# Units of TensorE with the same array shape side by side within each round of the first and last part

## The reference

```python
xs = jnp.fft.rfft2(x, axes=(1, 2)).reshape(B, H, W // 2 + 1, 8, 48)
xr, xi = jnp.real(xs), jnp.imag(xs)
o1r = relu(einsum('bxyhi,hio->bxyho', xr, w1[0]) - einsum(xi, w1[1]) + b1[0])
o1i = relu(einsum(xi, w1[0]) + einsum(xr, w1[1]) + b1[1])
o2r = einsum(o1r, w2[0]) - einsum(o1i, w2[1]) + b2[0]
o2i = einsum(o1i, w2[0]) + einsum(o1r, w2[1]) + b2[1]
out = irfft2(softshrink(o2r, 0.01) + 1j * softshrink(o2i, 0.01)) + x
```

## Time and profile before

| | |
|---|---|
| median of 3 runs | 995.19 us (990.65 to 997.57) |
| profiled execution, own time | 993.3 us |
| its span | 991.3 us |
| TensorE busy (matmul) | 916.0 us, 92% |
| VectorE busy | 577.1 us, 58% |
| ScalarE busy | 475.8 us, 48% |
| DMA | 184.41 MB, mean 186 GB/s |
| mean granted clock of TensorE | 0.976 |

### The profile page before, as it was taken

How to read it: one execution, slowest core, us unless ns; L and a number is a source line. 1 busy time by engine, 2 the same in 40 slices (tenths; PEclk the granted TensorE clock), 3 DMA queues, 4 the chain that set the end, 5 groups by cost and what they waited for, 6 DMA issues and landing times.

```text
span 991.3 us, 14302 instructions
## 1 busy us (share of the span) xinstructions
PE 916.0 (92%) x5168; PEld 460.3 (46%) x5168; DVE 577.1 (58%) x869; ACT 475.8 (48%) x757; POOL 81.1 (8%) x157
## 2 busy tenths in 40 slices
PE   2799999999999988999999999999999999999933
PEld 1555555665676655444444434444444444444411
DVE  1255555455454765787775676666666666666511
ACT  2455444444545424434343445565655656666521
POOL 3011111011111110000000101000000000000001
PEclk8899999999999999999999999999999999999986
DMA  9879699469648979856143443343654474554463
GB/s 283 324 206 298 202 282 366 150 180 283 248 136 269 260 237 277 210 138 164 48 114 95 112 127 108 108 123 113 213 170 129 153 247 134 161 156 153 142 192 128
DMA packets 95703, 184.41 MB, mean 186 GB/s; under 512 B 13007, under 2 KB 73769, under 8 KB 93842
## 3 DMA queue, kind: packets, MB, share of 16 engines
q1 hardware_dynamic: 85490, 143.65, 48.0%
q0 software_dynamic: 9696, 39.56, 12.4%
q10 hardware_dynamic: 448, 0.30, 0.1%
HBM read 104.32 MB, written 79.14 MB: 185 GB/s over the span
## 4 chain that ended last, share of the span: by engine, by line
PE 82%; DMA 9%; SPq 2%; DVE 2%; ACT 2%; issue 1%; POOL 0%; ACTq 0%; DVEq 0%
PE psum L948 17%; PE psum L957 16%; PE psum L987 8%; PE psum L1041 6%; PE psum L1065 6%; PE psum L1025 6%; DMA RG<-rows_along_h 6%; PE psum L936 5%; PE psum L967 5%; PE psum L998 4%; PE psum L1052 3%; PE psum L913 3%; PE psum L1014 2%; DMA rows_along_h<-RD 1%; SPq L611 1%
## 5 line engine op out<-in xcount | busy, mean ns | idle before, releaser
L1374 DVE SCALAR_TENSOR_TENSOR RA<-psum,RA 112x896 f32<-112x896 f32 (+1 forms) x120 | 124.1, 1035 | 206.3 <-ACT RA L1222 205.9
L1222 ACT ACTIVATE RA<-psum,small 112x896 f32<-112x896 f32 (+1 forms) x120 | 115.7, 964 | 94.7 <-PE psum L957 94.7
L957 PE MATMUL psum<-RA,RW 112*64 112x448 f32 (+1 forms) x640 | 131.1, 531 | 1.4 <-ACT RA L1213 1.4
L1213 ACT ACTIVATE RA<-psum,RW 112x448 f32<-112x448 f32 (+1 forms) x160 | 89.2, 609 | 80.0 <-PE psum L948 80.0
L1334 DVE COPY RD<-psum 128x672 f32<-128x672 f32 (+2 forms) x122 | 69.5, 571 | 58.3 <-PE psum L987 56.8
L987 PE MATMUL psum<-RD,const 128*128 128x384 f32 (+1 forms) x304 | 98.3, 445 | 3.7 <-DVE RD L1334 2.7
L1207 ACT ACTIVATE RA<-psum 128x384 f32<-128x384 f32 (+2 forms) x72 | 50.6, 702 | 78.9 <-PE psum L936 52.6
L936 PE MATMUL psum<-const,RX 128*112 128x128 f32 x528 | 68.5, 282 | 17.1 <-DMA RX<-rows_along_w 17.1
L1359 DVE TENSOR_TENSOR RX<-RX,RA 112x768 f32<-112x768 f32 (+2 forms) x80 | 80.8, 1011 | 2.5
L1207 ACT ACTIVATE RD<-psum 128x384 f32<-128x384 f32 (+2 forms) x122 | 64.0, 525 | 32.9 <-PE psum L987 30.9
L936 PEld LDWEIGHTS psum<-const,RX 128*112 128x112 f32 x528 | 61.2, 180 | 35.7 <-issue 34.9
(11 more groups left out here) (103 smaller groups left out, 1070.1 us busy)
## 6 DMA issues: line engine op xcount, KB each, us to landing
RG<-rows_along_h SPq DMA_DIRECT2D x7, 3072.0 KB, 11.5
RX<-x SPq DMA_DIRECT2D x16, 768.0 KB, 8.6
rows_along_w<-RX SPq DMA_DIRECT2D x54, 224.0 KB, 5.1
rows_along_h<-RD SPq DMA_DIRECT2D x84, 144.0 KB, 3.3
rows_along_h<-RD SPq DMA_DIRECT2D x56, 168.0 KB, 2.9
out<-RA POOLq DMA_DIRECT2D x12, 768.0 KB, 4.0
RX<-rows_along_w SPq DMA_DIRECT2D x12, 672.0 KB, 6.5
spectrum<-RA POOLq DMA_DIRECT2D x48, 168.0 KB, 4.7
```

Source lines behind the costliest of these rows:

```text
L957: mm = nc.tensor.matmul(bank[b * HALF:(b + 1) * HALF, a * BANK:a * BANK + nk * H], w4[layer][0:ROWS, g, b, a], hidden(slot)[0:ROWS, b * N: ...
L1213: done = nc.scalar.activation(hidden(slot)[0:ROWS, b * N:b * N + nk * H], banks(key)[0:ROWS, b, 0:nk * H], ACT.Relu, bias=bias[layer][0:RO ...
L1222: nc.scalar.activation(dst, src, ACT.Relu, bias=minus_lambda_l0 if key[0] == "S4" else minus_lambda).then_inc(act_emptied, 1)
L1374: nc.vector.scalar_tensor_tensor(out=dst, in0=src, scalar=LAMBDA / 64 if key[0] == "S4" else LAMBDA, in1=dst, op0=ALU.add, op1=ALU.min).th ...
```

## The change

Within each round of `order()` the units are put in another order, so that those of one kind are neighbours. Nothing else in the file is changed: the same 637 units, the same rounds (except `CI` of the last two items, one round earlier), the same DMA code.

- A, a round before: `S2 TA [S1] [6A] S3 5A S4 [S1] [6A]`; after: `S2 TA [6A 6A] 5A [S1 S1] S3 S4`.
- C, a round before: `3L2 5C 3L3 4L2 [6C] 4L3 TC [6C]`; after: `3L2 3L3 4L2 4L3 TC 5C [6C or 6C 6C]`.
- C, the `CI` units: `3L2(0) 4L2(0) 3L2(1) CI(8,0) 4L2(1) CI(8,1) 3L2(2) CI(9,0) 3L3(0) ...` before; `3L2(0) CI(8,0) CI(8,1) 4L2(0) 3L2(1) 4L2(1) CI(9,0) 3L2(2) 3L3(0) ...` after.

```diff
@@ -110,24 +110,18 @@
             o += [("S2", r)]
         if 0 <= r - 4 < ALL_STEPS:
             o += [("TA", r - 4)]
+        for p in range(PASSES - 1):
+            if 0 <= r - flip_round(p) < FLIP_UNITS:
+                o += [("6A", p, g, r - flip_round(p)) for g in range(PASS_PAIRS)]
+        if 0 <= r - 6 < 2 * ALL_GROUPS:
+            o += [("5A", (r - 6) // 2, (r - 6) % 2)]
         for p in range(1, PASSES):
             if 0 <= r - first_transform_round(p) < X_PARTS:
-                o += [("S1", p, 2 * (r - first_transform_round(p)))]
-        for p in range(PASSES - 1):
-            if 0 <= r - flip_round(p) < FLIP_UNITS:
-                o += [("6A", p, 0, r - flip_round(p))]
+                o += [("S1", p, 2 * (r - first_transform_round(p)) + v) for v in range(2)]
         if 0 <= r - 1 < ALL_STEPS:
             o += [("S3", r - 1)]
-        if 0 <= r - 6 < 2 * ALL_GROUPS:
-            o += [("5A", (r - 6) // 2, (r - 6) % 2)]
         if 0 <= r - 2 < ALL_STEPS:
             o += [("S4", r - 2)]
-        for p in range(1, PASSES):
-            if 0 <= r - first_transform_round(p) < X_PARTS:
-                o += [("S1", p, 2 * (r - first_transform_round(p)) + 1)]
-        for p in range(PASSES - 1):
-            if 0 <= r - flip_round(p) < FLIP_UNITS:
-                o += [("6A", p, 1, r - flip_round(p))]
         if r == PREP_ROUND:
             o += [("PR",)]
         if 0 <= r - ALL_STEPS - 4 < 2:
@@ -156,27 +150,23 @@
     for r in range(C_ROUNDS):
         if r < ALL_STEPS:
             o += [("3L2", r)]
-        if r == 1:
-            o += [("CI", ITEMS - 2, 0)]
-        elif r in (2, 3):
-            o += [("CI", ITEMS - 1, r - 2)]
+        if 0 <= r - L3_LAG < ALL_STEPS:
+            o += [("3L3", r - L3_LAG)]
+        if r == 0:
+            o += [("CI", ITEMS - 2, h) for h in range(2)]
+        if r < ALL_STEPS:
+            o += [("4L2", r)]
+        if 0 <= r - L3_LAG < ALL_STEPS:
+            o += [("4L3", r - L3_LAG)]
+        if r in (1, 2):
+            o += [("CI", ITEMS - 1, r - 1)]
+        if 0 <= r - L3_LAG - 1 < ALL_STEPS:
+            o += [("TC", r - L3_LAG - 1)]
         if 0 <= r - L3_LAG - 3 < 2 * ALL_GROUPS:
             o += [("5C", (r - L3_LAG - 3) // 2, (r - L3_LAG - 3) % 2)]
-        if 0 <= r - L3_LAG < ALL_STEPS:
-            o += [("3L3", r - L3_LAG)]
-        if r < ALL_STEPS:
-            o += [("4L2", r)]
-        if r == 1:
-            o += [("CI", ITEMS - 2, 1)]
         for p in range(PASSES - 1):
             if 0 <= r - last_inverse_round(p) < S1_UNITS // inverse_rate(p):
-                o += [("6C", p, inverse_rate(p) * (r - last_inverse_round(p)))]
-        if 0 <= r - L3_LAG < ALL_STEPS:
-            o += [("4L3", r - L3_LAG)]
-        if 0 <= r - L3_LAG - 1 < ALL_STEPS:
-            o += [("TC", r - L3_LAG - 1)]
-        if 0 <= r - last_inverse_round(PASSES - 2) < S1_UNITS // 2:
-            o += [("6C", PASSES - 2, 2 * (r - last_inverse_round(PASSES - 2)) + 1)]
+                o += [("6C", p, inverse_rate(p) * (r - last_inverse_round(p)) + v) for v in range(inverse_rate(p))]
     o += [("6C", PASSES - 1, v) for v in range(S1_UNITS)]
     return o
 
```

## The result

The changed kernel takes 999.55 us (median of 20 runs, 993.48 to 1006.37) where the kernel before takes 995.09 (20 runs, 990.65 to 1002.37): 1.0042 of its time, 95% interval 1.0025 to 1.006. Measured again later beside the kernel before it was 1.0065 (1.0036 to 1.0093). (One of its 12 later executions, 1009.88 us, counts as a slow one and is left out of that ratio.) It is slightly slower, by some 4 to 7 us, where the forecast was 7.4 us faster. The profiled execution took 1006.37 us (span 1004.4), 6.8 more than its median and the longest of the 20, so what is summed up from its trace is more than what a median run loses. A unit is named by its stage and step, so S4(38) is S4 of step 38. In the code of after, every line behind `order()` is 10 lower than before: L948 is L938, L957 L947, L967 L957, L987 L977, L998 L988, L1014 L1004, L913 L903, L624 L614, L642 L632, L1484 L1474.

What follows compares the result with a forecast made beforehand. TensorE's pass through its unit list was taken to bound A and C. Pairs' -23.0 us, less new waits, left A -6.4, B 0, C -1.0: -7.4 us, 985.9 us profiled, 987.8 against the median; range 977 to 999 us.

Steps and rivals of the forecast that it cites:

- The price of a change of kind: TensorE in A and C: each pair of neighbouring same-kind units saves 0.14 to 0.18 us, mostly taken as 0.15.
- the count (23.0 us): Changes of kind removed: 49 in A (7.3 us) and 97 in C (15.7 us), together 23.0 us saved.
- F-F pairs: Neighbouring units of kind F (such as S2 and TA, or 5C, 5A, 6A): 75 of the 146 new pairs.
- second rival: A and C: F-F pairs bring half or nothing, 993.4 to 999.1 us; chance 0.17.
- third rival: C: VectorE becomes the bound, every round waits and the kernel is slower, 1005 us; chance 0.13.
- the rule that the prediction set against itself: TensorE: a weight load runs beside matmuls only where row groups differ, so F-F pairs would be worth nothing.
- first rival: Whole kernel: all the saving is kept, nothing new waited for except 4.1 us for CI, 973.5 us; chance 0.14.
- +4.1 for CI: Start of C: CI(8,0) right behind 3L2(0) leaves TensorE idle 4.1 us for VectorE's additions.
- +3.2 for G: C: 6C waits 3.9 us for the load of G in passes 0 and 1, 3.2 us more than before together.
- +3.7 for the end of A: End of A: VectorE's additions delay copies and double banks behind the 6A pair, 3.7 us more; bounds 0 and 6.
- A's own signs: A in the changed profile: CF(0,0) 5 to 9 us earlier, 6A's waits for G gone (1.9 to about 0.2 us).
- it moves with them: End of C: the last 6C block's 16.7 us wait moves with the last 5C groups, whose stores and loads it awaits.

Runs made afterwards that it cites:

- experiment 5: Changed kernel with CI one round later, 6C of passes 0 and 1 one round later, and A's last-flip second 6A unit behind S4: 974.71 us, 0.9786 of before.
- experiment 3: 6C of passes 0 and 1 one round later: in the changed kernel 986.45 us, 0.9914; in the kernel before 989.77 us, 0.9948.
- experiment 2: Changed kernel with the CI units of the last two items one round later in C: 994.26 us, 0.9977 of the kernel before.
- experiment 4: Changed kernel with only the second 6A unit of A's last flip put behind S4 again: 995.97 us, 1.0011 of the kernel before.
- experiment 1: Kernel before with the new order in A alone: 992.04 us, 0.9957; with the new order in C alone: 1010.4 us, 1.0138.
- experiment 8: Changed kernel with CI, 6C and 6A edits, and 5C behind 3L2 in rounds 40 to 44: 971.68 us; also 5C third in 16 rounds with 6C: 969.87 us.
- experiment 6: Changed kernel with 5C third in C's rounds, near its old place, instead of behind TC: 986.99 us, 0.9905 of the kernel before.
- the three versions with all edits: Changed kernel with CI and 6C later, 6A apart: 974.71 us; also 5C behind 3L2 in rounds 40 to 44: 971.68; also 5C third in 16 rounds: 969.87.

## Why the prediction was wrong

What held. The price of a change of kind and the count (23.0 us) come out in experiment 5, within its some 2.5 us. The waits of the new order came where the text put them: CI(8,0) 4.18 us (forecast 4.1), 3L2 1.13, 0.81 and 0.77 twice (0.8 to 1.2 in three rounds of a pass; 5.4 us for 6.3), 4L3 0.8 longer twice, S4 and TA at the end of A 4.2 us (3.7), the first G 4.22 (3.9). The first G came late by 4.2 to 5.4 us in the five profiles with this C and 6C in its place, so the 3.9 was near but low. VectorE didn't become the bound of C, and F-F pairs are worth 0.17 with 5C, so neither the second nor the third rival came true, and the rule that the prediction set against itself doesn't hold for TC and 5C either (0.73 us for 0.82). That 999.1 us, the end of the second rival, is nearly the measured time is chance; it was reached by another way. The first rival's 973.5 us was to be had, but only with the waits edited out, before's two for G among them (974.7 and less).

What failed is a term that is missing: the step that priced a wait of TensorE at its own length (+4.1 for CI, +3.2 for G, +3.7 for the end of A). The two waits for G before had cost no more (experiment 3: 5.2 us for 4.9), and I carried this over to waits of 4 us. Behind those the clock fell: 13.7 us in the profiled execution, and by experiments 2 to 4 the four places were worth 22.4 us together (29.3 against the later ratio), where the forecast had 4.1 + 7.8 + 3.7 = 15.6 us in them.

The trace of before held the warning. My list of waits stopped at 360 us, and the longest wait of A ends at 360.08, timeline of TensorE and a window of 1 us:

```profile
360.08 2.42 PE L987 MATMUL psum<-RD,const 128*128 128x384 f32 x4 [2.69 <-DVE RD L1334]
```

```profile
361.00:362.00 1.00, 1.00 (x3) 0.67 (x2) 1.00 (x2) 0.00 (x0) 0.00 (x0) 0.50 1.07 415
```

The clock is at 0.50 from about 360.6 to 364.0 us there, and the unit takes 2.42 us where it takes 1.53 at full clock (experiment 1 and the kernel before with 6C later have it).

In us of a median run, estimated from the experiments, the 11.6 us between the forecast's -7.4 and the measured +4.2 are: 5.7 at the two G (experiment 3), 2.4 at CI (6.5 for 4.1), 2.1 in A (-4.3 for -6.4) and 2.5 at the end of the kernel, 12.7 together. A's own signs agree: CF(0,0) came 3.5 us earlier (358.78 for 362.30) and not 5 to 9, and 6A still waited 0.91 us for G, not 0.2.

Two smaller ones. The second G was not late by the same 3.9 us but by 3.76 to 7.35 in five profiles (7.35 and 5.03 in the changed kernel's two): I had its load at 11.3 us as before, and it took 15.2 and 12.9. And "it moves with them" for the last block of 6C: 5C at the end of its round bunches the last three units, and the end grew by 2.5 us (experiment 8 gives it back).

The range to 999 missed by 0.6 us. The bounds of the waits in it (G 6 us more, VectorE late) and the rivals at its upper end had no low clock in them.

Left open: why the same wait of 2.1 us of S4(38) is followed by the fall in five executions and not in the sixth; why the clock, once low at the second G, came back only 11 us after the start of work in four profiles (waits of 4.74 to 7.35 us) and after 3 to 7 us at the first G (4.22 to 5.36 us); and the last 1 to 3 us in the sums of experiments 5 and 6.

## What to carry over

A reorder is worth what its pairs save only as long as it makes no new idle time on TensorE: price every wait of some 4 us that it creates at about one and a half times its length here (at the second G it was up to twice), or move the waiting unit by one round first. Read the list of waits to the end of every stage, and look behind each whether the clock fell. Look for the loss in the granted clock and in the durations of equal units behind a wait, as no column of idle time shows it. A result that many later steps wait for (here 5C's for G) may stand early at the price of a few pairs, as in experiments 6 and 8.

## What the runs showed of the hardware

- **The clock behind a wait.** In 18 of 18 waits of 3.7 to 9.4 us within C (CI in six profiles, G in twelve places), the unit behind them ran at 1.2 GHz (CI's pair 7.01 to 8.25 us for 5.40, 6C 1.45 to 1.56 us for 0.88). Of the waits of 6C for G of 2.2 to 2.5 us none of two in the kernel before was followed by it, and both were with A changed alone. The clock was back 3 to 12 us behind the start of work, and the loss was some 1.6 to 5.7 us a place (estimated as half of that time).
- **Shorter waits.** The fall comes behind some of them. The last wait of A (2.38 to 2.70 us) was followed by it in 12 of 14 profiles, the kernel before's among them, the wait of S4(38) of 2.1 us in five of six, and one of 1.20 and one of 1.36 us of 6A for G were; waits of 1.40 and 1.71 us of 6A for G were not. So the length of the wait alone doesn't decide it.
- **Spread.** The changed kernel's 12 later runs lie within 16.3 us (14.6 without the longest), the five of each of the three versions with all edits within 2.0 to 3.2; five runs of the new C alone, with its three long waits, lie within 4.9. That the long waits make the spread is argued, not shown: the series have different lengths.
- **The array's shape.** Two neighbours of one kind together take 0.14 to 0.18 us less than with neighbours of another kind, read for pairs of all four kinds (Q-Q 1.44 us for two of 0.80), and the whole sum (-21.7 worked out, -21.3 measured) bears it out. That it is the shape, and not something else in which the kinds differ, no run separates.
